# Feed-forward half steps by another table, beside the attention of a one-core Perceiver kernel

## The reference

```python
x = x + L0_xattn(layernorm(x), ctx)   # softmax(q k^T / 16) v over 1601 keys, one head
x = x + L0_attn(layernorm(x))         # causal self-attention over 64 tokens, 64 features in q and k
x = x + L0_ffn(layernorm(x))          # quantised feed-forward, below
x = x + L1_xattn(layernorm(x), ctx)   # 16 heads over 1601 keys
x = x + L1_attn(layernorm(x))         # 16 heads, causal
x = x + L1_ffn(layernorm(x))          # top 2 of 8 experts
```

```python
def act_quant(x):                     # per token
    scale = 127.0 / clip(max(abs(x), axis=-1), 1e-5)
    return clip(round(x * scale), -128, 127) / scale
h = act_quant(x) @ ternary(w1).T      # 256 -> 1024
h = depthwise_conv1d(h, conv_w, conv_b)   # 3 taps along the 64 tokens
h = silu(h)
out = act_quant(h) @ ternary(w2).T    # 1024 -> 256
```

## Time and profile before

| what | value |
|---|---|
| runs | 2726.33, 2735.12, 2734.28 us; median 2734.28 |
| profiled execution | 2731.11 us, its span 2729.4 us |
| mean granted TensorE clock | 0.969 |
| PE, DVE, ACT, POOL busy | 92%, 62%, 50%, 31% of the span |
| tile steps with feed-forward | some 185 to 405 us of the span |
| tail | some 405 to 503 us |

### The profile page before, as it was taken

The page is one execution under the profiler, slowest core; times in us unless marked ns, Lnnn a source line. Parts: engine busy times, 40 slices in busy tenths (PEclk is TensorE's granted clock), DMA queues, the critical chain, the costliest instruction groups (busy, mean ns, idle before and its releaser), DMA issues.

```text
span 2729.4 us, 75620 instructions
## 1 busy us (share of the span) xinstructions
PE 2522.3 (92%) x32404; PEld 2169.6 (79%) x32404; DVE 1702.9 (62%) x3035; ACT 1377.1 (50%) x2201; POOL 836.4 (31%) x857
## 2 busy tenths in 40 slices
PE   6999886789999999999999999999999976999997
PEld 3566556678888888888888888888888855999997
DVE  3467778436566565575665655756756555777775
ACT  1233434445565555555555555555556523555563
POOL 1010003333344434433434344344343300111111
PEclk9999997899999999999999999999999976999999
DMA  9876740460011001100100011001001102666664
GB/s 345 314 307 266 284 178 25 145 212 26 26 42 38 30 30 38 42 30 26 49 31 30 30 38 42 30 26 54 26 30 40 55 2 99 211 200 206 207 202 145
DMA packets 61265, 283.47 MB, mean 104 GB/s; under 512 B 5137, under 2 KB 36242, under 8 KB 46354
## 3 DMA queue, kind: packets, MB, share of 16 engines
q1 hardware_dynamic: 52818, 268.73, 27.5%
q0 software_dynamic: 8160, 10.29, 2.5%
HBM read 247.45 MB, written 33.65 MB: 103 GB/s over the span
## 4 chain that ended last, share of the span: by engine, by line
PE 55%; DVE 13%; issue 13%; DMA 7%; POOL 7%; ACT 4%; SPq 0%; POOLq 0%; DVEq 0%; ACTq 0%
PE PS L1439 7%; PE PS L1275 5%; PE PS L1263 5%; DVE mpart L1809 3%; PE PS L1184 3%; PE PS L1252 3%; PE PS L1250 3%; PE PS L1251 3%; POOL ctx_lo L603 3%; PE PS L1435 3%; DMA unit_raw<-in_experts 3%; DMA sum_d<-scaled,xg 2%; POOL k_lo L595 2%; PE PS L1241 2%; DMA ctx_raw<-in_ctxT 2%
## 5 line engine op out<-in xcount | busy, mean ns | idle before, releaser
L1809 DVE TENSOR_REDUCE mpart<-PS 128x1 f32<-128x802 f32 (+1 forms) x512 | 484.7, 986 | 213.8 <-PE PS L1263 212.8
L921 ACT ACTIVATE probs<-PS 128x1024 f32<-128x1024 f32 (+1 forms) x416 | 413.4, 1025 | 217.8 <-PE PS L1439 217.8
L603 POOL TENSOR_TENSOR ctx_lo<-ctx_raw,ctx_hi 128x801 fp32r<-128x801 f32 x128 | 225.9, 1775 | 375.0 <-ACT ctx_hi L856 366.4
L595 POOL TENSOR_TENSOR k_lo<-probs,k_hi 128x400 fp32r<-128x400 f32 (+1 forms) x256 | 250.8, 980 | 275.2 <-ACT k_hi L844 275.2
L1439 PE MATMUL PS<-qbd_hi,k_hi 64*128 64x256 f32 (+1 forms) x1664 | 313.6, 374 | 0.0
L1263 PE MATMUL PS<-k_hi,qbd_hi 128*128 128x512 f32 (+2 forms) x1024 | 265.5, 361 | 22.7 <-DVE mpart L1809 12.7
L843 ACT COPY probs<-PS 128x400 f32<-128x400 f32 (+1 forms) x256 | 126.4, 494 | 244.7 <-PE PS L1243 215.3
L1275 PE MATMUL PS<-probs,vals 128*32 128x64 f32 x13312 | 233.8, 221 | 4.2 <-issue 4.0
L1250 PE MATMUL PS<-wkv_hi,ctx_hi 128*128 128x256 f32 (+1 forms) x832 | 236.5, 284 | 0.0
L1439 PE MATMUL PS<-qbd_lo,k_hi 64*128 64x256 f32 (+1 forms) x1664 | 234.5, 278 | 2.0 <-issue 2.0
L1439 PE MATMUL PS<-qbd_hi,k_lo 64*128 64x256 f32 (+1 forms) x1664 | 234.3, 278 | 0.0
(11 more groups left out here) (319 smaller groups left out, 6250.8 us busy)
## 6 DMA issues: line engine op xcount, KB each, us to landing
unit_raw<-in_experts SPq DMA_DIRECT2D x46, 1536.0 KB, 7.0
ctxN<-in_ctxN SPq DMA_DIRECT2D x16, 3328.0 KB, 11.0
ctxT<-in_ctxT SPq DMA_DIRECT2D x16, 3204.0 KB, 11.3
ctx_raw<-in_ctxT SPq DMA_DIRECT2D x64, 801.0 KB, 4.5
slots_d<-pad_rows SPq DMA_DIRECT2D x18, 1040.0 KB, 12.4
xg<-slots_d SPq DMA_DIRECT2D x23, 260.0 KB, 2.8
x<-in_x SPq DMA_DIRECT2D x1, 2048.0 KB, 10.1
sum_d<-x SPq DMA_DIRECT2D x1, 2048.0 KB, 13.8
```

Of the source, the lines that this page charges most:

```text
L595: g.tensor_tensor(k_lo[:, n, a, c:c + width], k_raw[p % 2][:, 0:width], k_hi[:, n, a, c:c + width].bitcast(F32), ALU.subtract).then_inc(s. ...
L603: g.tensor_tensor(ctx_lo[:, a, cols], ctx_raw[:, cols], ctx_hi[:, a, cols].bitcast(F32), ALU.subtract).then_inc(s.ctx_lo_ready, 1)
L921: act.activation(probs[rows, t % PROBS, :], PS[rows, 1024 * (t % 2):1024 * (t % 2) + 1024], ACT.Exp).then_inc(s.pr_ready, 1)
L1809: v.tensor_reduce(mpart[:, pair, half:half + 1], PS[:, at:at + width], AX, ALU.max).then_inc(s.mx_red, 1)
```

## The change

Scaling of the hidden chunk with its row scales goes from half step 17 to 16, the output product and the addition from 18 to 17, and the maximum of the first 128 tokens from 13 to 14, where that of the second is. The products with the diagonals now write bank 0 instead of bank 3. ACT's copy of the row scales becomes a function of its own, `copy_rows`, which stands ahead of the exponential in an attention step. The number of half steps falls by one.

```diff
-FFN_STEPS = 4 * CHUNKS + 15
+FFN_STEPS = 4 * CHUNKS + 14
...
@@ ACT, ffn
-                for f in chunk_at(step, 17):
-                    act.wait_ge(s.rows_ps, f + 1)
-                    act.copy(rowscale[:, :], bank(3, CHUNK)).then_inc(s.rows_ready, 1)
...
+            def copy_rows(step):
+
+                for f in chunk_at(step, 16):
+                    act.wait_ge(s.rows_ps, f + 1)
+                    act.copy(rowscale[:, :], bank(0, CHUNK)).then_inc(s.rows_ready, 1)
+
             def act_pair_a(i):
                 first, last = i == 0, i == TILES - 1
                 if not first:
                     copy_xsT()
+                copy_rows(2 * i)
                 act.wait_ge(s.nmax_ready, T["nmax"].up())
...
@@ ACT, behind tile 15
             act.copy(wkv_hi[:, :, :].rearrange("p k n -> p (k n)"), wkv_raw).then_inc(s.wkv_hi_ready, 1)
+            copy_rows(2 * TILES)
             copy_qkv()
...
             for step, beside in BESIDE_FFN:
+                copy_rows(step)
                 ffn(step)
...
@@ PE, ffn: behind the hidden products, ahead of piece 8
+                for f in chunk_at(step, 16):
+                    pe.wait_ge(s.diag_ready, TPC * (f + 1))
+                    for k in range(TPC):
+                        mm = pe.matmul(bank(0, P, at=k * P), ones[:, :], diag[:, k, :], start=True, stop=True)
+                    mm.then_inc(s.rows_ps, 1)
...
                 for f in chunk_at(step, 17):
-                    pe.wait_ge(s.diag_ready, TPC * (f + 1))
-                    for k in range(TPC):
-                        mm = pe.matmul(bank(3, P, at=k * P), ones[:, :], diag[:, k, :], start=True, stop=True)
-                    mm.then_inc(s.rows_ps, 1)
-                for f in chunk_at(step, 18):
                     pe.wait_ge(s.hq_ready, f + 1)
...
@@ DVE, ffn
+                for f in chunk_at(step, 16):
+                    scale_hidden(f)
                 for f in chunk_at(step, 17):
-                    scale_hidden(f)
-                for f in chunk_at(step, 18):
                     add_ffn(f)
...
-                    for f in chunk_at(step, 13 + k):
+                    for f in chunk_at(step, 14):
                         hidden_max(f, k)
```

## The result

The changed kernel took **2760.97 us** (median of 4 runs, 2755.95 to 2763.77) beside 2734.49 for the kernel before in the same comparison: a ratio of 1.0098, 95% interval 1.0086 to 1.0110. It is 26.5 us slower. The forecast was 2746 in a range of 2730 to 2757: the direction was right, the size was less than half, and the range was missed by 4 us.

The account below looks back on a forecast made before the run. PE was taken to bound even tile steps, DVE's late scores' maximum the odd ones. Tile part +5.5 and tail +6 gave +11.5 on 2731.11, 2742.6 for the profiled execution, 2746 on the median; range 2730 to 2757.

Parts of the forecast that it names:

- Odd steps, -4.5 each: Tile steps 9, 11, 13: less DVE work ahead of the scores' maximum saves 4.5 us each.
- Even steps, 1.8 + 2.4 + 1.3 = 5.5 each: Tile steps 8, 10, 12, 14: three uncovered terms lengthen each by 5.5 us, +22.0 together.
- lead: End of scores to the probabilities' transposes: row-scale copy ahead of the exponential makes it 1.8 us later in even steps.
- middle: Probabilities' transposes to attention output's transposes: scaling on DVE makes PE wait 2.4 us more in even steps.
- end: Attention output's transposes to end of next scores: output products replace row-scale products on PE, +1.3 us in even steps.
- a rival with a price of 1.3 a time: PE falls to half rate in the new waits, eight times: +10 us, 2756; chance 0.13.
- The tail, +6: Half steps 32 to 45, up to the second part: later last row-scale copy costs 6 us, bounds 0 and 10.
- (a): Tail: the first row-scale copy stands ahead of the q, k, v copies, about 1.2 us.
- (b): Tail: the addition follows its output product with little or nothing between to cover it, 1.9 to 5.4 us.
- (c): Tail, half steps 36 and 40: ACT's row-scale copy ahead of its centre taps delays DVE's side taps, 2.0 us twice.
- The tail absorbs its part: Rival: PE's pieces or the last load's wait set the tail, so +6 or a little less, 2740; chance 0.20.
- the middle is covered: Rival: DVE's longer work in even steps makes no PE wait; 2728.6 with the tail at 0; chance 0.12.

Follow-up runs that it names:

- filler: Changed kernel plus matmuls nobody reads ahead of PE's wait for the divided output, from tile step 7 on; 2751.93 us, ratio 1.0062 to the kernel before.
- filler_copy: Changed kernel with the same unread matmuls and ACT's row-scale copy behind the exponential in the tile steps; 2744.31 us, ratio 1.0034 to the kernel before.
- tail_copy: Changed kernel with ACT's row-scale copy behind its centre taps, only behind half step 32; 2758.82 us, ratio 1.0094 to the kernel before.
- tail_max: Changed kernel with the first activation maximum of chunks 5 to 7 back in half step 13; 2758.08 us, ratio 1.0090 to the kernel before.
- mending the three places: Changed kernel, tail only: maxima apart again, row-scale copy behind ACT's other copies, diagonal products behind quantised x's transposes; 2749.13 us, ratio 1.0048.
- tiles_new: Kernel before with the new table only for chunks 0 to 3, scaled in the tile steps; 2748.09 us, ratio 1.0052.
- tail_new: Kernel before with the new table only for chunks 4 to 7, scaled in the tail; 2746.06 us, ratio 1.0045.
- quantise_behind: Changed kernel with quantising of x behind the self-attention's addition in the tile steps; 2733.53 us, ratio 0.9997 to the kernel before.

## Why the prediction was right or wrong

The profiled execution took 2755.95 us where the sum gave 2742.6 for it, 13.4 more: 5.4 in the tile steps, 7.4 in the tail, 0.6 behind them.

- **Odd steps, -4.5 each:** measured -4.3 (28.0 to 23.7), three times. Right. Tile 15 up to its attention transposes: -3.4 against -3.45. Step 7: +0.6 against +0.5.
- **Even steps, 1.8 + 2.4 + 1.3 = 5.5 each:** right at full clock: step 10 and step 14 grew by 5.5, and all four in filler. The single terms hold too, by step 10 of both traces: lead 6.48 instead of 4.74, +1.7 against 1.8; middle 12.07 instead of 9.65, +2.4 against 2.4; end 9.91 instead of 8.53, +1.4 against 1.3. PE's wait for the exponential is 1.61, as the prediction's "about 1.6". filler_copy prices the copy's place at 1.73 a step.
- **The failed step in the tiles** was to add the sum at full clock: what of DVE's middle is longer "is paid in full", and nothing more was added behind that wait. The wait of 2.3 us costs itself and, in some of the steps, the rate of what follows, the 16 output products above all: +2.85 in step 8 and +1.64 in step 12. These 4.5, and 0.6 that the odd steps saved less, make most of the way from +5.5 to +10.8. The working named this as a rival with a price of 1.3 a time, twice that at the output product, in eight places. The price was near where it struck (1.64, and 2.85 at the output product); it struck twice in this execution, in the wait for the division and never in the one for the exponential. It was given 0.13 and belonged with the forecast, as an addition of some 3 to 8 us: in the trace of the kernel before, three waits for the exponential of 2.73 to 2.77 us (steps 9, 11, 13) had the clock down behind them, and the "against" rested on the one in tile 15 that had not the earlier trace rows.
- **The tail, +6, was mis-sized:** +13.4, beyond the upper bound of 10. By term: (a) the first copy ahead of q, k, v, 1.2: the mask of the self-attention came 3.2 later behind T15 (17.1 us instead of 13.9); in filler, where the clock doesn't fall behind that tile's division, it is 15.3, so 1.4 are this term and 1.8 the clock, down behind the 3.14 us wait for tile 15's division. (b) The uncovered output product, 1.9 to 5.4: 4.7 between the side taps of chunk 7 and the last copy. (c) The copy ahead of the centre taps, 4.0: tail_copy gives back 0.3, so the copy's place was nearly nothing. DVE does wait for the centre taps of half step 40, 3.72 us, but they come late for another reason: PE had stood 3.45 us (to 485.40) for both maxima ahead of its transposes, and the hidden products follow behind these; with the maxima apart again (tail_max) the two waits are 1.64 and 2.13. The filling of 3.04 us of idle time, -3.0: scaling fills that gap, but nothing is won by it. DVE waits 3.17 us ahead of it (1.89 before), and 1.96 and 3.37 behind it, where it waited 0.17 or not at all. The sum had both maxima in one half step only as lost cover for the product in (b); tail_max prices them at 3.8, part of it through (b). Not in the sum at all were the products with the diagonals at half rate ahead of the next transposes (1.22 instead of 0.61, about 1.3 with what they push), and GpSimd's remainders beside the first scaling (last section), some 1.2. What mending the three places leaves, 104.9 less 100.6, is 4.3: (a), its clock, and what is left of the others.
- **The tail absorbs its part; the middle is covered:** both out. The wait for the divided output was there in each even step.
- **What was argued only:** the split of the tail between (b), the maxima, the half-rate products and GpSimd's share is read from starts in the traces; the runs price the maxima alone and all three mends together, not each share.

The Trainium skill (TensorE: Matmul & The Clock Gate, section What's actually happening) says that the throttled state is the default and that the monitor behind it runs on its own, without regard to where a kernel starts. The traces fit that and don't prove it: equal waits of 2.26 and 2.27 us ended one at half and one at full rate; tail_copy and tail_max lost their time in steps 8 and 12 like the changed kernel, while tiles_new, with the same instructions in these steps and step 7 begun 0.8 us later, lost it in 8, 9, 10 and 14.

## What to carry to other kernels

Moving work from ahead of one wait to ahead of the next helps only as far as the engine has cover at the second: count that cover first, and look for another piece (here quantising, 2.2 us) that can leave the place where the moved one arrives; that turned a loss of 26 us into none, and with the copy behind the exponential and the tail left alone into a gain of 11. Add to every new wait of TensorE the price of what comes behind it at half rate, with a chance by place: here the clock fell behind waits of 1.4 to 3.2 us, not behind every one, and at other steps in other versions with the same instructions. It costs most where TensorE sets the pace behind the wait. A table that serves a dense stretch and a sparse tail should be costed in each by itself, in the tail along the one chain that sets its end.

## What the hardware showed beyond that

Matmuls that nobody reads, put ahead of a wait, kept the clock at 1.00 over the whole stretch of 195 us and made the kernel 9 us faster by median (in the profiled executions 5.1 up to T15 and 1.5 in the tail) although PE had more to do.

Some of DVE's smallest operations took eight to eleven times as long when GpSimd was at work. The timelines of POOL and DVE of the changed kernel, in the tail:

```profile
457.75 1.90 POOL L608 TENSOR_TENSOR qbd_hi<-q_hi,head_of 128x1024 fp32r<-128x1024 f32 x1
459.60 1.90 POOL L608 TENSOR_TENSOR qbd_lo<-q_lo,head_of 128x1024 fp32r<-128x1024 f32 x1
```

```profile
457.83 1.84 DVE L1702 TENSOR_SCALAR small<-small 128x2 f32<-128x2 f32 x1
459.70 0.17 DVE L1703 RECIPROCAL small<-small 128x2 f32<-128x2 f32 x1
459.79 1.74 DVE L1705 TENSOR_SCALAR small<-small 128x2 f32<-128x2 f32 x1
```

Two operations on 128x2 numbers, 0.17 and 0.21 elsewhere, end when GpSimd's end: 3.2 us on the way to the scales of chunk 5. The Trainium skill (SBUF — State Buffer, section Who interferes with whom) says that DVE and GpSimd share a pair of ports, that TENSOR_SCALAR can take it and that the second to issue stands still for the whole instruction. The rows agree, and a row shows that the reciprocal between them (0.17) didn't wait. The kernel before had the same two (1.84 and 1.74), so they are no part of the difference.

Large operations are, a little. In the tail the new table puts the first scaling beside GpSimd's remainders of the next context. The timelines of DVE and POOL of the changed kernel:

```profile
433.59 3.60 DVE L1715 TENSOR_TENSOR hidden_f<-hidden_f,rowscale 128x2048 f32<-128x2048 f32 x1
437.23 2.52 DVE L1716 TENSOR_SCALAR hq<-hidden_f 128x2048 bf16<-128x2048 f32 x1
```

```profile
433.44 5.21 POOL L603 TENSOR_TENSOR ctx_lo<-ctx_raw,ctx_hi 128x801 fp32r<-128x801 f32 x2 [5.65 <-ACT ctx_hi L860]
```

In step 8 the same two took 2.28 and 1.23, so this place cost 2.6 us; in the kernel before the remainders met the quantising of x and cost 1.4 (1.67 instead of 0.40 at its first operation). tail_new, tail_max, quantise_behind and filler show the same 3.60. DVE has no wait from the mask to the layer norm there, so the difference of some 1.2 us is part of the tail's 13.4; no run here takes it away alone.
